# Row gathers with a bounds check for edge columns that hold no edge, and a masked last chunk, in a two-layer graph attention network on one core

## The reference

```
x += graph attention 0 (8 heads of 32; score = a_src.h[src] + a_dst.h[dst] + sum(relu(edge_attr @ edge_W.T + b) * h[dst]))
x += a slice-attention FFN
x += graph attention 1 (8 heads; score = (x @ W_u.T + b_u)[src] + (x @ W_v.T)[dst]; messages are rows of x)
x += mixture of 8 experts, top 2, hidden size 1024
```

```python
alpha = jnp.where(alpha >= 0, alpha, 0.2 * alpha)
amax = jax.ops.segment_max(alpha, dst, num_segments=n)
ex = jnp.exp(alpha - amax[dst])
denom = jax.ops.segment_sum(ex, dst, num_segments=n)
out = jax.ops.segment_sum(h_src * (ex / denom[dst])[..., None], dst, num_segments=n)
```

## Time and profile before

| | |
|---|---|
| time of the whole program, 3 runs | 4079.53, 4085.51, 4096.33 us; median 4085.51 |
| the profiled execution: span, first to last instruction | 4086.3 us, 69498 instructions (its own time is not listed beside it) |
| busy in the span: TensorE matmul, weight load | 2989.6 us (73%), 2168.3 us (53%) |
| VectorE | 2289.9 us (56%) |
| ScalarE | 1298.0 us (32%) |
| GpSimd (POOL) | 2301.6 us (56%) in 2343 instructions |
| granted TensorE clock, mean | 0.875 |
| HBM traffic | 430.09 MB read, 57.50 MB written, 119 GB/s |

### The profile page before, as it was taken

The page is one execution under the profiler, slowest core; times in us unless marked ns, Lnnn a source line. Parts: engine busy times, 40 slices in busy tenths (PEclk is TensorE's granted clock), DMA queues, the critical chain, the costliest instruction groups (busy, mean ns, idle before and its releaser), DMA issues. The chain is left out here.

```text
span 4086.3 us, 69498 instructions
## 1 busy us (share of the span) xinstructions
PE 2989.6 (73%) x12787; PEld 2168.3 (53%) x12788; DVE 2289.9 (56%) x5023; ACT 1298.0 (32%) x5485; POOL 2301.6 (56%) x2343
## 2 busy tenths in 40 slices
PE   4623777787878887999666665665656489999998
PEld 3422444444444444667544444444444378898887
DVE  4533888888888887874355555555555611111111
ACT  1401444444444454432211111111111533333343
POOL 5156777777777773002577777777777623333332
PEclk9866999899999998998777777778777789999999
DMA  8635444344444442000244444444444756666564
GB/s 188 193 89 147 116 116 117 105 108 108 108 107 109 110 111 62 0 2 30 75 112 113 113 112 113 112 113 113 113 112 112 220 173 166 170 174 167 167 172 128
DMA packets 292188, 487.96 MB, mean 119 GB/s; under 512 B 145315, under 2 KB 193393, under 8 KB 291625
## 3 DMA queue, kind: packets, MB, share of 16 engines
q0 software_dynamic: 127312, 325.41, 32.1%
q1 hardware_dynamic: 155936, 158.55, 13.2%
q10 hardware_dynamic: 8880, 3.34, 0.4%
HBM read 430.09 MB, written 57.50 MB: 119 GB/s over the span
## 5 line engine op out<-in xcount | busy, mean ns | idle before, releaser
L902 POOL DMA_INDIRECT g_rows<-rows,g_recs x1856 | 1764.1, 950 | 628.9 <-issue 474.1
L947 PE MATMUL g_pA<-g_msg,k_ident 128*128 128x264 f32 (+1 forms) x3712 | 1150.2, 463 | 474.0 <-DVE g_pA L1141 409.4
L947 PEld LDWEIGHTS g_pA<-g_msg,k_ident 128*128 128x128 f32 x3712 | 805.4, 228 | 803.8 <-issue 659.1
L936 PE MATMUL g_pE<-g_ew,g_recT 128*128 128x512 f32 x932 | 511.8, 676 | 251.3 <-DVEq L1125 248.4
L1135 DVE TENSOR_TENSOR g_msg<-g_rows,g_pp 128x1024 f32 (+3 forms) x464 | 571.9, 1233 | 151.2 <-DVEq L84 151.1
L1985 POOL DMA_INDIRECT out<-e_ys,e_goal x102 | 160.7, 1576 | 501.8 <-issue 481.1
L936 PEld LDWEIGHTS g_pE<-g_ew,g_recT 128*128 128x128 f32 x932 | 170.0, 202 | 468.9 <-DVEq L1125 343.1
L2038 PE MATMUL e_pY<-e_w,e_hT 128*128 x1632 | 373.8, 382 | 30.3 <-issue 30.3
L1057 ACT ACTIVATE g_pp<-g_dd 128x32 f32<-128x32 f32 x464 | 95.2, 205 | 921.0 <-ACTq L84 921.0
L2027 PEld LDWEIGHTS e_pH<-e_xT,e_w 128*128 128x128 f32 x3264 | 382.9, 193 | 5.2
L2027 PE MATMUL e_pH<-e_xT,e_w 128*128 128x128 f32 x3264 | 383.2, 276 | 0.0
(11 more groups left out here) (418 smaller groups left out, 3446.2 us busy)
## 6 DMA issues: line engine op xcount, KB each, us to landing
e_w<-in_L_ffn_W SPq DMA_DIRECT2D x110, 1024.0 KB
g_rows<-rows,g_recs POOLq DMA_INDIRECT x1856
g_recs<-slots SPq DMA_DIRECT2D x468, 8.0 KB
tok<-e_xall SPq DMA_DIRECT2D x7, 910.0 KB
rows<-p_row SPq DMA_DIRECT2D x50, 119.0 KB
own<-p_row SPq DMA_DIRECT2D x50, 119.0 KB
p_x<-in_x SPq DMA_DIRECT2D x1, 5600.0 KB
own<-p_x SPq DMA_DIRECT2D x1, 5600.0 KB
```

What stands on the lines that cost most here:

```text
L902: pool.indirect_dma_start(out=rows[:, r, j, :], out_offset=None, in_=rows_d, in_offset=bass.IndirectOffsetOnAxis(ap=recs[:, r, 4 * j:4 * j ...
L936: last = t_.matmul(pE[:, c:c + 512], recT[:], ew[:].rearrange("p c d -> p (c d)")[:, c:c + 512], start=True, stop=True)
L947: last = t_.matmul(sums, K["ident"][:], of, start=False, stop=(j == C - 1), skip_group_check=True)
```

## The change

Columns in which no node of the tile has an edge get the index 2N in all their slots instead of N, and the row gathers get a bounds check at NPAD - 1 that skips such indices silently. A skipped row leaves in the buffer what was there, so the four row buffers are cleared once per layer, and in each tile's last chunk -1e30 is added to the score of every slot at or beyond the node's degree. For this, sort_nodes lays out two more values on all partitions, `full` = 4(c - 1) and `top` = max(largest degree, 9), and windows builds from `full` a table `shut` of 49 x 4 values per partition. Some scratch tiles now share memory with others.

```diff
@@ sort_nodes
+        diag_b = at_t[0:QT, 0, 0:2, :]
...
-        deep = m.sb("o_deep", [1, QT])
-        aim = m.sb("o_aim", [1, QT])
-        reach = m.sb("o_reach", [1, QT])
+        deep = tq[0:1, 0:QT]
+        aim = posf[0:1, 0:QT]
+        reach = pq[0:1, 0:QT]
...
                 ch.link(v.tensor_scalar(cf[:], ci[:], 3.0, None, ALU.max))
+                v.tensor_scalar(fullc[:], cf[:], float(C), -float(C), ALU.mult, ALU.add)
+                v.tensor_scalar(deepest[:], dmax[:], float(2 * C + 1), None, ALU.max)
...
+                ch.wait()
+                v.tensor_scalar(diag_b[:, 0, :], K["ident"][0:QT, 0:QT], fullc[:], None, ALU.mult)
+                ch.link(v.tensor_scalar(diag_b[:, 1, :], K["ident"][0:QT, 0:QT], deepest[:], None, ALU.mult))
...
+                v.tensor_copy(K["full"][:], pB[:, 0:QT])
+                v.tensor_copy(K["top"][:], pB[:, QT:2 * QT])
...
+                t_.matmul(pB, K["ones"][0:QT, :], diag_b.rearrange("p a t -> p (a t)"), start=True, stop=True)
                 t_.matmul(pD[:, 0:QT], K["ones"][0:QT, :], diag[:], start=True, stop=True).then_inc(pre_ok, 1)
@@ windows
-            pool.memset(tailw[:, :, 0], N).then_inc(tail_ok, 1)
+            pool.memset(tailw[:, :, 0], 2 * N).then_inc(tail_ok, 1)
...
+            kc = Chain(dve, bch)
+            kc.link(v.tensor_tensor(K["shut"][:], over(iota_c, 1, QT), over(K["full"][:], 2, C), ALU.add))
+            kc.link(v.tensor_tensor(K["shut"][:], K["shut"][:], over(K["deg"][:], 2, C), ALU.is_ge))
+            kc.link(v.tensor_scalar(K["shut"][:], K["shut"][:], -BIG, None, ALU.mult))
...
-                ch.link(v.tensor_tensor(mk[:], over(K["iota64"][:, 0:WIN * C], 1, GT), over(K["deg"][:, ts], 2, WIN * C), ALU.is_ge))
+                v.tensor_tensor(mk[:], over(K["iota64"][:, 0:WIN * C], 1, GT), over(K["deg"][:, ts], 2, WIN * C), ALU.is_ge)
+                ch.link(v.tensor_tensor(void[:], over(K["iota64"][:, 0:WIN * C], 1, GT), over(K["top"][:, ts], 2, WIN * C), ALU.is_ge))
+                ch.link(v.tensor_tensor(mk[:], mk[:], void[:], ALU.add))
                 dve.wait_ge(win_in[g], 16 * GT)
                 src = win[:, ts, :, 0]
                 v.scalar_tensor_tensor(src, mk[:], float(N), src, ALU.mult, ALU.max).then_inc(masked, 1)
@@ graph
-                        if not first:
+                        if first:
+                            pool.wait_ge(blank, r + 1)
+                        else:
                             pool.wait_ge(msg_ok, 4 * (u - 1) + (r + 1))
                             pool.sem_inc(pace, 1)
...
-                                                    in_offset=bass.IndirectOffsetOnAxis(ap=recs[:, r, 4 * j:4 * j + 1].bitcast(I32), axis=0)
-                                                    ).then_inc(rows_in[r], 16)
+                                                    in_offset=bass.IndirectOffsetOnAxis(ap=recs[:, r, 4 * j:4 * j + 1].bitcast(I32), axis=0),
+                                                    bounds_check=NPAD - 1, oob_is_err=False).then_inc(rows_in[r], 16)
...
+                for r in range(R):
+                    v.memset(rows[:, r, :, :], 0.0).then_inc(blank, 1)
                 v.memset(al[:], 0.0).then_inc(w_zero, 1)
...
+                    if closes:
+                        ch.link(v.tensor_tensor(heads(sc), heads(sc), over(row_of(K["shut"][:, bass.ds(t, 1), :]), 2, H), ALU.add))
                     ch.link(v.scalar_tensor_tensor(sc, sc, 0.2, sc, ALU.mult, ALU.max))
@@ slice_ffn, stage f2
-            q = m2.sb("f2_q", [G, INNER])
-            k_ = m2.sb("f2_k", [G, INNER])
+            qk = m2.sb("f2_qk", [G, 2, INNER])
+            q, k_ = qk[:, 0, :], qk[:, 1, :]
...
-            oz = m2.sb("f2_oz", [G, FH, 128])
+            oz = qk[:].rearrange("g a (h c) -> g (a h) c", c=128)
...
-                    v.memset(oz[:], 0.0)
...
                     v.tensor_tensor(g3(at[:]), g3(pq[:]), over(red[:], 2, G), ALU.subtract).then_inc(exp_in, 1)
+                    v.memset(oz, 0.0)
                     dve.wait_ge(exp_out, 1)
@@ experts
-            both = m2.sb("e0_both", [Q, QT, X])
+            both = K["sdst"]
```

More of the change, by code:

```diff
@@ L222, in sort_nodes @@
         diag = m.sb("o_diag", [QT, QT])
+        fullc = m.sb("o_fullc", [QT, 1])
+        deepest = m.sb("o_deepest", [QT, 1])
+        diag_b = at_t[0:QT, 0, 0:2, :]
         tail = m.sb("o_tail", [1, 4], I32)
         spare = m.sb("o_spare", [1, QT])
-        deep = m.sb("o_deep", [1, QT])
-        aim = m.sb("o_aim", [1, QT])
-        reach = m.sb("o_reach", [1, QT])
+        deep = tq[0:1, 0:QT]
+        aim = posf[0:1, 0:QT]
+        reach = pq[0:1, 0:QT]
         shallow = m.sb("o_shallow", [QT, 1])
@@ L237, in sort_nodes @@
         pC = pM[0:1, 256:448].rearrange("p (a c) -> p a c", a=3)
+        pB = pR[:, 256:256 + 2 * QT]
         banks = (pH[0][:], pH[1][:], pTt[:], pR[0:P, :], pT[0][0:P, 0, :])
@@ L455, in _ @@
                 v.tensor_copy(K["end"][:], pC[:, 0, QT:QT + 1])
[L456 to L461, removed]
+                ch.link(v.tensor_scalar(reach, pC[:, 2, 0:QT], -3.0, None, ALU.add))
+                v.scalar_tensor_tensor(K["pl"][:], pC[:, 0, 0:QT], 8.0, reach, ALU.mult, ALU.add)
+                ch.link(v.tensor_scalar(deep, pC[:, 2, 0:QT], float(WIN - 1), None, ALU.is_ge))
+                ch.link(v.scalar_tensor_tensor(aim, pC[:, 0, 0:QT], 3.0, spare[:], ALU.add, ALU.subtract))
+                ch.link(v.tensor_tensor(aim, aim, deep, ALU.mult))
+                v.tensor_tensor(K["dc"][:], aim, spare[:], ALU.add)
                 ch.link(v.tensor_scalar(tail[:, 0:1], pC[:, 0, QT:QT + 1], 3.0, None, ALU.add))
@@ L606, in windows @@
     mk = m.sb("x_mk", [Q, GT, WIN * C])
+    void = m.sb("x_void", [Q, GT, WIN * C])
     tailw = m.sb("x_tailw", [Q, WIN * C, 4], I32)
@@ L617, in windows @@
     ew_zero = T("ew_zero"); zeroed = T("zeroed"); tail_ok = T("tail_ok"); tail_out = T("tail_out"); mch = T("mch"); pace = T("pace")
+    bch = T("bch"); iota_c = K["iota64"][:, 0:C]
     kset = T("kset"); xch = T("xch"); midx_ok = T("midx_ok"); more_in = T("more_in"); more_ok = T("more_ok"); more_out = T("more_out"); stored = T("stored")
@@ L829, in graph @@
         rec_in = [S(f"rec_in{r}") for r in range(R)]; rows_in = [S(f"rows_in{r}") for r in range(R)]
-        rows_ok = S("rows_ok"); w_zero = S("w_zero"); pace = S("pace"); cch = S("cch"); fch = S("fch")
+        blank = S("blank"); rows_ok = S("rows_ok"); w_zero = S("w_zero"); pace = S("pace"); cch = S("cch"); fch = S("fch")
         recT_ps = S("recT_ps"); recT_ok = S("recT_ok"); enc_ok = S("enc_ok"); enc_free = S("enc_free"); lane_ok = S("lane_ok")
@@ L1516, in _ @@
                     dve.wait_ge(toV, 3)
-                    v.tensor_copy(q[:], pq[:])
-                    v.tensor_copy(k_[:], pk[:])
+                    v.tensor_copy(q, pq[:])
+                    v.tensor_copy(k_, pk[:])
                     v.tensor_copy(vv[:], pv[:]).then_inc(toP, 1)
@@ L2157, in program @@
              "deg": m.sb("k_deg", [Q, QT]), "ct": m.sb("k_ct", [1, QT + 2], I32),
-             "lt": m.sb("k_lt", [1, QT], I32), "wt": m.sb("k_wt", [1, QT + 3], I32), "cap": m.sb("k_cap", [Q, QT]), "end": m.sb("k_end", [1, 1], I32), "pl": m.sb("k_pl", [1, QT], I32), "dc": m.sb("k_dc", [1, QT], I32)}
+             "lt": m.sb("k_lt", [1, QT], I32), "wt": m.sb("k_wt", [1, QT + 3], I32), "cap": m.sb("k_cap", [Q, QT]), "end": m.sb("k_end", [1, 1], I32), "pl": m.sb("k_pl", [1, QT], I32), "dc": m.sb("k_dc", [1, QT], I32),
+             "full": m.sb("k_full", [Q, QT]), "top": m.sb("k_top", [Q, QT])}
         def scratch(name, shape, dt=F32):
@@ L2167, in program @@
         K["x"] = m.sb("k_x", [Q, QT, D])
+        K["shut"] = m.sb("k_shut", [Q, QT, C])
         K["sdst"] = m.sb("k_sdst", [Q, QT, H])
```

## The result

| | runs | median | lowest to highest |
|---|---|---|---|
| before | 4 | 4088.37 us | 4079.53 to 4096.33 |
| changed | 4 | 4138.59 us | 4134.14 to 4141.56 |

The ratio is 1.0125, 95% interval 1.0114 to 1.0137: slower by 50 us by the medians. The time is 41 us above the forecast of 4098. It lies outside the forecast's own range of 4085 to 4106 and inside the wide one of 4060 to 4240; it is the place of rival 1, a check that costs POOL time on every gather.

What follows compares the result with a forecast made beforehand. POOL's gather queue was taken to bound layer 1, VectorE most of layer 0. Mask 12 + 0.5, set-up 1.2, FFN -0.6, check and void gathers 0: about +13 on 4086.3, forecast 4098 us; own range 4085 to 4106, eight-in-ten 4060 to 4240.

Steps and rivals of the forecast that it cites:

- rival 1: Row gathers: the check costs POOL time on every one; total 4136 us at 0.04 us each, 4253 at 0.11; chance 0.43.
- What bounds the layers: Layer 1 is POOL's gather queue, 1.256 us a gather; layer 0 is bound on VectorE's side in 46 of 49 tiles.
- the prediction's sum for layer 0 over the 49 tiles: Layer 0: the larger of VectorE's and POOL's time per tile, added over all tiles, comes to 1220 us.
- the 39 us of room: Layer 0: POOL's queue needs 1181 us of the 1220, so it absorbs the first 0.04 us per gather.
- The bounds check: All 1856 row gathers: taken as 0 on POOL, at most 0.62 us each; called the weakest step.
- The prediction's own sign of being wrong: Row gathers: wrong if L902's median moves by 10 ns, or if layer 1 shrinks by over 30 us.
- The void gathers: Both layers: 152 of 1856 gathers find every index out of bounds; POOL's saving on each taken as 0.
- My assumed deal of rows to queues: Indirect DMAs: 106 rows over 2 queues, 128 over 16; 13.6 ns a step, 0.11 us for the eight steps.
- The mask: Last chunk of each tile: one more VectorE operation, 49 x 0.24, +12 us in layer 0; covered in layer 1, +0.5 at ends.
- Clearing the buffers: Start of each layer: four memsets of 1.15 us, 4.6 us together, taken as 0; at most 4.6 twice.
- Set-up: Chain to the first window gather: small added operations, diagonals and copies, +1.2 us; mask-table operations covered, 0.
- FFN: FFN stage: the 0.91 us memset leaves the head and returns beside the exponential, -0.9 + 0.3 = -0.6 us.

Runs made afterwards that it cites:

- run 1: The kernel before with nothing but the bounds check on the row gathers, no index out of bounds: 4149.92 us, ratio 1.0154.
- run 3: The changed kernel with index N in the void slots, so that the check never fails and no row is skipped: 4142.4 us, ratio 1.0144.
- run 4: The changed kernel as it is, repeated on the second chip: 4140.58 us, ratio 1.0129 to the kernel before.
- run 2: The changed kernel without the bounds check, void slots again gathering row N; mask, clearing, set-up and FFN edits stay: 4083.59 us, ratio 0.9991.
- run 6: The kernel before with a never-failing bounds check on own rows, window gathers, new-row scatters and token gathers, not on the row gathers: 4101.69 us, one run.
- run 5: The changed kernel with the row gathers' bound in layer 1 set to 0, skipping nearly all its rows: 4109.64 us, one run; experts get other tokens.
- run 7: The changed kernel without the check, void columns not gathered at all: POOL and SP read an index and branch: 3992.6 us, ratio 0.9781.

## Why the prediction was right in its range and wrong in its case

**What bounds the layers: right, and it carried the rest.** Layer 1 is POOL's queue: 928 x 0.052 is 48 us, and the four traces with the check on every row gather show +43.5 to +46.2 in it against the trace of before, and +46.1 to +47.6 on one chip (runs 1, 3 and 4 against run 2). With 1.303 us for a gather the prediction's sum for layer 0 over the 49 tiles gives 1230 us instead of 1220, +10; run 1 measured +12.2. Of the 48 us that the check adds to POOL there (928 x 0.052), 36 disappear in the 39 us of room.

**The bounds check: the step that failed.** "Of the check I take 0." It is 52 ns on the row gathers. The step reasoned from the likeness of the plain gathers to each other, which says what bytes cost and nothing about a check. The likeness was itself a choice of lines: two plain gathers of the same trace are not within 10 ns of 950.

```profile
L1972 POOL DMA_INDIRECT e_xs<-tok,e_at x102 | 100.3, 983 | 48.3 <-issue 41.3 <-DVE e_wgt L2111 6.1 <-PE e_pX L2010 0.9
L338 POOL DMA_INDIRECT p_drow<-in_dst,p_blk_i x50 | 60.5, 1209 | 48.3 <-DVE p_drow L357 35.2 <-issue 9.2 <-DVE p_blk_i L352 4.0
```

The step also explained the 0.62 us of the accumulating scatter by the read of its destination. In run 6 the check on a plain scatter is worth 21 ns, so nearly all of the 0.62 us is something else, as the step said; that it is that read, no run shows. But 0.008 us was enough to decide, and no row of the trace could bound the check as closely as that. The prediction's own sign of being wrong, a median of L902 that moves by 10 ns, came true five times over: 949 to 1002. That the time still lies in the wide range is owed to rival 1, whose chance of 0.43 was as large as the forecast's. Rival 1 had the mechanism and the place; its case at 0.04 us was 4136 us, and the measured 0.052 would have made it 4086 + 12 + 49 = about 4147 with its own terms, 8 above the measured time; the stretch after the last gather came out 8.6 shorter.

**The void gathers: right.** Taken as 0; the least of all gathers is 6 ns under the median, and with the whole layer void there is still nothing (run 5). What had said so beforehand were the two scatters with 117 and 83 skipped rows. My assumed deal of rows to queues is left unsupported: writing fewer of them changed nothing, so the 0.11 us for eight steps is not the cost of rows that are really written. By the Trainium skill, page "DMA: Bandwidth & Descriptors", section "Anatomy of one DMA — SWDGE (gpsimd) path", the part of such a DMA that varies is bytes over 436 GB/s. Taken for POOL's side, that would be an estimated 0.32 us less for each of 928 gathers of run 5, 297 us. The trace disagrees: 1209.3 us against 1208.2 in run 4. The same section of the Trainium skill calls the generation of descriptors small and variable. The trace shows POOL busy 0.95 us on a plain row gather, and layer 1 consists of that and of the 0.30 us between two.

**The mask: right place, size too large.** +12 us predicted in layer 0, +4.9 measured (run 2), 0.10 us a tile instead of 0.24. The operation itself was priced too low (0.33 us in the median closing chunk), and it was charged in full; but VectorE waits at the next tile's opening, and 0.23 us went into that wait. In layer 1 the mask is hidden, as predicted: no gather of that layer in run 2 starts later than 0.35 us after the one before it has ended.

**The small terms.** Clearing the buffers: 0 predicted, and the traces agree. Line 924's group above names the memset L1130 as a releaser, but at the start of layer 0 that memset had ended two microseconds before the gather:

```profile
353.54 0.96 DVE L1130 MEMSET g_rows<- 128x1088 f32 x1 [7.59 <-PEq L113]
353.80 1.77 SPq L885 DMA_DIRECT2D g_recs<-slots  x4
...
356.45 1.02 POOL L924 DMA_INDIRECT g_rows<-rows,g_recs  x1 [12.96 <-DVE g_rows L1130]
```

The gather starts 2.65 us after the loading of the records does, and it was 2.49 before. The memsets take 0.96 us each and start 1.14 apart, where 1.15 was priced.

Set-up: +1.2 predicted. The start of layer 0 cannot show it, since the first gather starts anywhere between 354.2 and 357.5 us over the traces of before, after and runs 1 to 4, and at 357.0 in run 1, which has no set-up. The chain itself can: from the reduction of `o_dmax` to the index operation at the head of the windows VectorE takes 8.27 us in the changed kernel and 6.60 before, +1.67. The wait for TensorE's product in it grew from 1.02 to 1.92 us. The lines of before, then those of the changed kernel:

```profile
230.69 0.28 DVE L436 TENSOR_REDUCE o_dmax<-o_pM 49x1 f32<-49x128 f32 x1
...
237.29 0.21 DVE L699 TENSOR_SCALAR x_idx<-k_rp 128x49 int32<-128x49 f32 x1 [1.09 <-PEq L113]
```

```profile
229.36 0.28 DVE L440 TENSOR_REDUCE o_dmax<-o_pM 49x1 f32<-49x128 f32 x1
...
233.97 0.21 DVE L461 COPY k_cap<-o_pM 128x49 f32<-128x49 f32 x1 [1.92 <-PE o_pM L593]
...
237.63 0.21 DVE L713 TENSOR_SCALAR x_idx<-k_rp 128x49 int32<-128x49 f32 x1 [1.09 <-PEq L113]
```

FFN: -0.6 predicted. VectorE's timeline of stage f2 in run 2:

```profile
1824.59 1.42 DVE L1448 COPY f_sums<-f_pTok 128x257 f32<-128x257 f32 x4 [3.00 <-PE f_pS L1353]
1826.81 0.17 DVE L1529 TENSOR_SCALAR f_rn<-f_sums 128x4 f32<-128x4 f32 x1 [0.79 <-PEq L113]
...
1840.53 0.68 DVE L1540 COPY f_tok<-f_pq 64x512 f32<-64x512 f32 x1 [8.32 <-PE f_pq L1493]
...
1852.18 0.91 DVE L1548 MEMSET f_qk<- 64x1024 f32 x1 [0.16 <-issue]
```

From the sums' copy to `f_tok` it is 15.94 us where it was 17.89, -2.0. About 1 us more than the memset's own 0.91 was gained, and no run says why. Bytes: 21 MB predicted and seen.

**The sum.** Predicted +13: mask 12, check 0, the others +1. In the spans it is +51.9: check 46 in layer 1, 12 in layer 0, mask 5 there, the gap between the layers -4 (429.6 to 433.9 us over the four traces with this FFN, so partly spread), the start +1, the stretch of the experts -9 (spread and perhaps the change, as said above). Of the +13, the 12 of the mask and the 1 of the rest are not borne out by the whole either: run 2 is 3.5 us faster than before.

## What to carry to other kernels

Where one engine's queue of equal instructions is the whole length of a stage, price an argument added to that instruction as unknown, and ask from what cost on it decides: here 8 ns of 950 would have. Count what a saving takes away in the currency of the engine that sets the time: skipped rows save bytes on DMA engines that were half idle, and what saved time on POOL was an instruction that is not issued. Then a register read and a branch, hidden as long as POOL's queue is full, bring 2% where the check lost 1.25%.

## What the runs showed of the hardware that was not expected

- A bounds check that nothing fails adds 49 to 52 ns of POOL time to an indirect gather of 128 rows with 512, 1088 or 2112 bytes a row, 64 to the token gathers, and 21 to a scatter of 128 rows (medians, runs 1 and 6).
- An indirect gather whose rows are nearly all skipped takes 998 ns of POOL, as one that moves all of them does, while the traffic falls from 99 to 2 GB/s (run 5).
- POOL can read an index from SBUF and branch on it once for each four gathers without losing its 1.25 us pace while its queue is full; after a wait for VectorE the gather starts 1.40 to 1.42 us behind the message instead of 0.81 (run 7).
